# A norm tail shared by two engines, reordered loads and value parts, and a pause ahead of scatter and gather DMAs

## The reference

```
xn = layernorm(x)
s  = (sigmoid(LN(xn Wq + bq) LN(xn Wk + bk)^T / 16 - log 2048) (xn Wv + bv)) Wo + bo, times layerscale
f  = routed(xn) + shared(xn)      # 16 experts, top 4 of them per row after a choice of 2 groups of 4; shared: 2 x 128 wide
x  = x + s * silu(f)
xn = layernorm(x)
s  = gelu(sqrt(2048) * (xn K^T) / norm(xn K^T)) V           # bank of 2048 keys and values
f  = gelu(xn ternary(W1)^T + b1) ternary(W2)^T + b2
x  = x + s * silu(f)
```

## Time and profile before

| what | value |
|---|---|
| three runs | 1225.1, 1225.28, 1227.74 us; median 1225.28 |
| the profiled execution | 1224.77 us, span 1223.0 us |
| PE busy | 1193.8 us, 98% of the span |
| DVE, ACT, POOL busy | 69%, 45%, 35% |
| mean granted clock of TensorE | 0.995 |
| DMA | 169.14 MB, 138 GB/s |

### The profile page before, as it was taken

One profiled execution on the slowest core, in us unless ns is written; L12 is line 12 of the kernel. 1 busy time (PEld: TensorE's weight loads), 2 busy tenths in 40 slices (PEclk: granted clock), 3 DMA queues, 4 the chain that ended last, 5 costly groups with the idle time before them and its releaser, 6 DMA issues.

```text
span 1223.0 us, 26541 instructions
## 1 busy us (share of the span) xinstructions
PE 1193.8 (98%) x8888; PEld 853.5 (70%) x8889; DVE 845.1 (69%) x1821; ACT 555.4 (45%) x1054; POOL 426.4 (35%) x376
## 2 busy tenths in 40 slices
PE   5899999999999999999999999999999999999998
PEld 4566566676788888866666667777766666666665
DVE  8697966556556555578899899999765545554554
ACT  6545732333466666665333345677542222222221
POOL 3353777777027360055777752212000000000000
PEclk8999999999999999999999999999999999999999
DMA  9488355454297666522566647541111101101100
GB/s 297 169 340 326 114 163 178 159 188 132 78 286 241 199 194 193 171 83 74 150 212 199 183 151 234 171 139 53 53 52 53 34 19 53 52 8 43 52 18 18
DMA packets 137830, 169.14 MB, mean 138 GB/s; under 512 B 12899, under 2 KB 126710, under 8 KB 135446
## 3 DMA queue, kind: packets, MB, share of 16 engines
q1 hardware_dynamic: 114438, 125.49, 31.6%
q0 software_dynamic: 12368, 33.70, 8.7%
q10 hardware_dynamic: 10944, 8.92, 2.3%
HBM read 84.18 MB, written 83.89 MB: 137 GB/s over the span
## 4 chain that ended last, share of the span: by engine, by line
PE 81%; DVE 11%; issue 4%; ACT 2%; DVEq 1%; DMA 1%; SPq 0%; ACTq 0%
PE bank L1220 28%; PE sums L1276 17%; PE sums L1235 12%; PE bank L1139 8%; PE sums L1149 4%; PE bank L1081 3%; PE bank L1119 3%; DVE stat L1890 2%; PE sums L1091 1%; DVE reg_w L2169 1%; PE sums L1072 1%; PE bank L1184 1%; PE bank L1057 1%; DVE reg_e L2159 1%; DVEq L1893 1%
## 5 line engine op out<-in xcount | busy, mean ns | idle before, releaser
L2169 DVE TENSOR_SCALAR reg_w<-reg_w 128x512 f16<-128x512 f32 x320 | 147.2, 460 | 197.8 <-ACT reg_w L1664 196.9
L1845 DVE SCALAR_TENSOR_TENSOR reg_w<-reg_w 128x512 f16<-128x512 f32 x320 | 222.4, 695 | 11.0
L1276 PE MATMUL sums<-reg_v,reg_w 128*128 128x256 f16 x1536 | 188.3, 273 | 0.0
L1235 PE MATMUL sums<-reg_v,reg_w 128*128 128x256 f16 x1536 | 188.1, 273 | 0.1
L1220 PE MATMUL bank<-reg_qk 128*128 (+1 forms) x768 | 186.6, 379 | 0.0
L1220 PE MATMUL bank<-reg_qk,kbT 128*128 128x512 f16 (+1 forms) x768 | 186.6, 379 | 0.0
L1664 ACT ACTIVATE reg_w<-bank 128x512 f32<-128x512 f32 x128 | 76.4, 597 | 241.8 <-PE bank L1220 241.8
L1276 PEld LDWEIGHTS sums<-reg_v,reg_w 128*128 128x128 f16 x1536 | 150.3, 98 | 44.3
L1235 PEld LDWEIGHTS sums<-reg_v,reg_w 128*128 128x128 f16 x1536 | 150.1, 98 | 44.3 <-DVE reg_w L1845 1.1
L1664 ACT ACTIVATE reg_w<-bank,nlogs 128x512 f32<-128x512 f32 x128 | 87.9, 687 | 162.5 <-PE bank L1220 157.6
L864 POOL DMA_INDIRECT reg_e<-yg_d,slot_i x128 | 131.0, 1023 | 45.7 <-issue 34.7
(11 more groups left out here) (244 smaller groups left out, 1646.9 us busy)
## 6 DMA issues: line engine op xcount, KB each, us to landing
xg_d<-kbT SPq DMA_DIRECT2D x18, 1024.0 KB, 4.9
xin<-xg_d SPq DMA_DIRECT2D x72, 256.0 KB, 2.9
yg_d<-xr SPq DMA_DIRECT2D x72, 256.0 KB, 2.2
reg_qk<-in_L_attn_x_dram SPq DMA_DIRECT2D x8, 512.0 KB, 7.5
sh_d<-xin SPq DMA_DIRECT2D x16, 256.0 KB, 2.4
xr<-xn_d SPq DMA_DIRECT2D x32, 128.0 KB, 2.4
reg_e<-sh_d SPq DMA_DIRECT2D x32, 128.0 KB, 2.8
moe_d<-reg_e SPq DMA_DIRECT2D x32, 128.0 KB, 1.9
```

What stands on the lines that cost most here:

```text
L1235: mm = pe.matmul(sums[:, bass.ds((c & 1) * (2 * 512) + q * D, D)], (ah, al)[x][:, j % 4, q * P:(q + 1) * P], m.second(y, j), start=(j == 0 ...
L1276: mm = pe.matmul(a_bank[2 * i + q // 2][:, (q % 2) * D:(q % 2 + 1) * D], part[:, j % 4, q * P:(q + 1) * P], m.second(y, j), start=(j == 0 ...
L1845: ins = dve.scalar_tensor_tensor(out=out_ap, in0=in_ap, scalar=scale, in1=hi_ap, op0=ALU.mult, op1=ALU.subtract)
L2169: dve.tensor_scalar(ah[:, j % 4, :], att[:, j % 2, :], m.split, None, ALU.mult).then_inc(m.hi_done, 1)
```

## The change

Four edits:

1. Norm tail. Of chunk 7's four blocks ACT normalizes two, and DVE the other two (`last_norm`), between weight block 6 and chunk 6. The high and low parts of weight block 7 (wpT) come behind those of chunk 7, together with block 8 (`splits_of`). PE's `route(5)` comes behind the transposes of chunk 7, with `route(6)` and `route(7)`.
2. SP issues the load of chunk 3 ahead of Wo, Wv and bv.
3. In each batch's projection the low parts of v of tiles 14 and 15 come behind the loop.
4. POOL executes a semaphore increment (`tile_seen`, which nothing waits for) between a tile's wait and its four DMAs, in `scatter` and in `gather`.

```diff
+        splits_of = slots_of[:NCH - 2] + [[], [WP_SLOT, BIAS_SLOT]]
+        tile_seen = sem("tile_seen")
...
             load(st_wk, rows(a["L0_attn_Wk"]), "qk")
+            load_x_all(3)
             load(st_wo, rows(a["L0_attn_Wo"]), "o_v")
             load(st_wv, rows(a["L0_attn_Wv"]), "o_v")
             load(bvf[:, :], a["L0_attn_bv"].rearrange("(t p) -> p t", p=P), "vb", allow_slow_non_contiguous=True)
-            load_x_all(3)
...
             def scatter(c):
                 pool.wait_ge(xr_ld[c % 4], 16 * (c // 4) + 16)
+                pool.sem_inc(tile_seen, 1)
                 for k in range(TOPK):
                     scatter_row(c, k)
...
             def gather(c):
                 pool.wait_ge(cb_step, TOPK * (c - YR + 1) + CR)
+                pool.sem_inc(tile_seen, 1)
                 for k in range(TOPK):
                     gather_row(c, k)
...
-                if c:
+                if 0 < c < NCH - 2:
                     route(c - 1)
-            route(NCH - 1)
+            for c in range(NCH - 3, NCH):
+                route(c)
...
-                for m in range(G4):
+                for m in range(G4 if c < NCH - 1 else 2):
                     ins = act.activation(xn4[c % 4][:, m, :], x_all[:, c, m, :], ACT.Identity,
                                          bias=nmr[:, i, m:m + 1], scale=rstd[:, i, m:m + 1])
...
-                for s in slots_of[c]:
+                for s in splits_of[c]:
                     weights_hi(s)
...
+            def last_norm():
+                c = NCH - 1
+                i = c % 2
+                dve.wait_ge(ln["xn"], at(2 * c))
+                for m in (2, 3):
+                    ins = dve.tensor_scalar(xn4[c % 4][:, m, :], x_all[:, c, m, :], rstd[:, i, m:m + 1],
+                                            nmr[:, i, m:m + 1], ALU.mult, ALU.add)
+                ins.then_inc(ln["xn"], 1)
...
-                for s in slots_of[c]:
+                for s in splits_of[c]:
                     weights_lo(s)
+                if c == NCH - 3:
+                    last_norm()
...
-                def row_moments(t, i):
+                def row_moments(t, i, values=True):
                     dve.wait_ge(pj["mm"], at(first_t + t))
                     dve.wait_ge(pj["qkn"], at(first_t + t - 2))
                     moments(lambda m: s_bank[i % 4][:, m * D:(m + 1) * D], 2, i % 2, first_t + t, pj, EPS * QK_PS * QK_PS)
+                    if values:
+                        values_lo(t, i)
+
+                def values_lo(t, i):
                     dve.wait_ge(pj["vhi"], at(first_t + t))
...
                     if more or i < 2:
-                        row_moments(t + 2, i + 2)
+                        row_moments(t + 2, i + 2, more)
...
                 by(dve, S // P, 4, rows_lo)
+                for i in (2, 3):
+                    values_lo(S // P - 4 + i, i)
```

## The result

The change took 1223.79 us (median of 19 runs, 1223.12 to 1225.29), the kernel before 1225.28 (19 runs, 1224.82 to 1227.74): ratio 0.9982, 95% interval 0.9975 to 0.9989, faster by 1.3 to 3.1 us. The medians differ by 1.49 us and the two profiled executions by 1.30 (1224.77 to 1223.47). Forecast were 1.4 us and 1223.9. Ten of before's runs lie at 1224.8 to 1225.3 and nine at 1226.1 to 1227.7; of the change's, one lies above 1224.3. So the ratio, by which the gain is 2.2 us (0.0018 of 1226), says more than the medians.

A forecast was written before the change was run, and what follows sets the result against it. PE, busy for 98% of the span, was taken as the bound. Terms -1.4 + 0 + 0 + 0 from 1224.77 gave 1223.4 us profiled, 1223.9 as a median, with a range of 1222.0 to 1226.8.

The forecast's parts named there:

- Part 1: Norm tail: DVE's idle time filled and wpT's low part moved behind chunk 7's, forecast -1.4 us, bounds 0.6 to 1.6.
- the cut of 0.1 for a late PE: Norm tail: 0.1 us taken off the 1.49 us gain because chunk 7's high parts had only 0.1 to spare.
- Part 2: Opening loads: chunk 3 comes sooner, but DVE then waits for chunk 4; forecast 0, bounds -0.67 and 0.
- Part 3: Projection's end: moving the last two value tiles' low parts leaves holes on DVE; forecast 0, -0.84 to +0.1 per batch.
- Part 4: POOL's semaphore pause ahead of each tile's four scatter or gather DMAs: forecast 0, between -0.28 and +0.30 us each.
- the 0.30 that I had as the upper bound: POOL's scatters and gathers: most one pause was taken to cost, in us, if it pays a second DMA gap.
- the room that I had counted: Gathers: 3.4 us before DVE's use of rstd plus 3.4 in POOL's waits, less 0.84, to absorb pause lag.
- my formula: Gathers: pause lag added over 28 tiles, free up to (3.4 + 3.4 - 0.84) / 28 = 0.21 us each.
- The sign I named for a wrong forecast: POOL's gap at a tile's first DMA exceeding 0.5 us, one of three listed signs.
- gathers falling behind: Rival at DVE's shift: pauses of 0.30 us outrun the room by 2.4, time 1226.3 us; chance 9%.
- "lost gain" rival: A low-clock stretch falls on the shared expert's first matmuls, costing up to 1.7 us, time 1225.6; chance 14%.
- value and load rivals: Projection waits shrink, 1222.2 us, chance 12%; the earlier load of chunk 3 pays too, 1223.2 us, chance 8%.

The follow-up runs named there:

- e1: The norm tail edit alone on the kernel before: ratio 0.9994 (0.9973 to 1.0015).
- e7: The whole change run again, at a time when PE was held back: ratio 0.9912 to the kernel before (0.9878 to 0.9946).
- e9: The whole change with the semaphore instruction behind each gather tile's first DMA instead of ahead of it: ratio 0.9985 to the kernel before.
- e2: The kernel before with only chunk 3's load moved ahead of Wo, Wv and bv: ratio 1.0004 (0.9979 to 1.0030).
- e3: The kernel before with only the low parts of the last two value tiles moved behind the projection loop: ratio 0.9997 (0.9973 to 1.0020).
- e11: The whole change plus scatters waiting for the tile before last, gathers waiting for the tile before, and chunk 4 loaded behind chunk 3: 1297.82 us, ratio 1.0585.
- e6: The kernel before with only chunk 3's load moved ahead of Wo, Wv and bv, sent a second time: ratio 1.0013 (0.9996 to 1.0031).
- e12: The whole change plus each tile's scatter waiting until those of the tile before last have landed: 1224.13 us, ratio 0.9978 to the kernel before.
- e10: The whole change plus each tile's scatter waiting until those of the tile before have landed: 1316.07 us, ratio 0.9216 to the kernel before.
- e4: The kernel before with only the semaphore instruction added ahead of each tile's scatters and gathers: ratio 0.9934 (0.9906 to 0.9961).
- e8: The whole change without the semaphore instruction: ratio 1.0009 to the kernel before (0.9982 to 1.0036).

## Why the prediction was right

**Part 1, -1.4 us: right, in place and size.** The chain is 1.23 us shorter at 41.46 and again at 58.17; with chunk 4's statistics 0.19 us later in this one execution, the tail itself gave 1.42. One term was mis-sized: DVE's two norm operations took 0.72 us on the chain (0.74 busy) and not 0.56; the 128x255 operations of the earlier trace rows were too cheap a neighbour. The four low parts took 2.40 there instead of 2.50. Together that is 3.12 for 3.06, so the working without the cut of 0.1 for a late PE would have given 1.43. The cut was not needed in this execution, and too small in e1, e7 and e9: that 1.4 and 1.42 agree so closely is partly luck.

**Part 2, 0: right**, for the reason given: chunk 4's landing sets DVE's next step (17.45 before, about 17.65 after). e2 shows it alone.

**Part 3, 0: right**, the hole doesn't close, since DVE waits for ACT's high part (e3).

**Part 4, 0: right in the sum, wrong in its working.** I priced an instruction between two DMAs and found what I took: the gap stays 0.30, also at the first DMA of 26 of the 28 gather tiles. I missed that the tile's wait moves from the DMA to that instruction. At a blocked tile this costs 0.53 us of restart and 0.4 of slower DMAs, above the 0.30 that I had as the upper bound. It didn't matter because only the first tile was blocked, and the room that I had counted took the lag up: the waits for DVE at the later tiles fell from 5.5 us to 2.2, and the last gather's rstd began at 721.72, 0.62 sooner than before where all else was 1.3 sooner, with DVE's use 2.7 us behind its end instead of 3.4. So about 0.7 us of lag was left of the first tile's, inside the room, and none was added per tile as my formula had it. The sign I named for a wrong forecast, a gap above 0.5, did occur, in the restart of the blocked tile, without a cost to the end. That the pause gains 10 us while PE is held back was nowhere in the prediction.

**The rivals.** That gathers falling behind reach the end is right as a mechanism, and e11 shows the price to within 0.4 us at DVE's shift; the pause is far from it. The low clock of the "lost gain" rival exists, with 1.68 us where the rival had 1.7, but it fell on the other side. In the nine profiles with the tail none had it at the shared matmuls (in three it took 0.45 a little earlier); in the five without the tail one had (e6). It could be what sets before's nine runs at 1226.1 to 1227.7 apart, but one in five is no proof, and a larger share of before's runs lies up there: nine of 19, and with e11 and e12 eight of 9 and ten of 13. A late load of chunk 4 (e3: 1.6 us) and the step at 130 us (0.5 to 0.7, in e1 and e10 over 4) move runs as far. The value and load rivals fell.

**The number.** The prediction's 1.4 is what one traced execution of each kernel shows, 1.30. The runs say 2.2 (1.3 to 3.1) and, with e12, 2.5. The part above 1.3, some 0.9 us, is in no term of the sum and in no trace; the forecast median came out to 0.1 us because it started from 1225.28, which is the top of before's lower group. What share the low clock, the late load and the step have in it stays open, since only one execution of each kernel was traced.

## What to carry to other kernels

Work moved into another engine's idle time pays where the chain says so, and in full only if the engine behind it (here PE with its transposes) keeps pace: at the lower clock a third of the gain was lost. Ask of a wait which instruction it stands on, not only how many instructions there are: an instruction put behind a wait takes the wait over. Before adding a cost up over all steps, ask at which of them it is paid: here one restart was paid, and the waits of later steps took it up, while a wait for each step's landing was paid 28 times and came out at the end (e11). And when runs differ by more than the effect sought, trace more than one execution of each kernel.

## What the runs showed of the hardware

- DVE's norm, a TENSOR_SCALAR of 128x256 with two scalars per row, took 0.37 us (two in 0.74); the 128x255 ones of the earlier trace rows took 0.28.
- A semaphore instruction ahead of an indirect DMA is free while nothing blocks (0.30 both ways); after a block the DMA starts 0.81 us behind its releaser instead of 0.27 (27 tiles of e4 and e7 against 28 of e8 and e9).
- The Trainium skill, page Perfetto Trace Analysis, section DMA Instruction — SWDGE (GPSIMD), has the sequencer ready for the next instruction once it has pushed such a DMA into the wait queue. The trace agrees: in the change the second tile's semaphore instruction ran at 574.2, while the first tile's third gather ran (573.32 to 574.45) and ahead of its fourth (574.76), and the gap of 0.30 stayed.
- In nine of the kernels (e1 to e9) PE got one matmul through in 2.8 us (median from 165 to 295 us) while indirect scatters ran one behind the other at a pitch of 1.27, in e3 for instance:

```profile
205.44 0.37 PE L1235 MATMUL sums<-reg_v,reg_w 128*128 128x256 f16 x1 [2.43 <-issue]
205.84 0.96 POOL L847 DMA_INDIRECT xg_d<-xr,slot_i  x1 [0.30 <-issue]
207.10 0.96 POOL L847 DMA_INDIRECT xg_d<-xr,slot_i  x1 [0.30 <-issue]
208.24 0.37 PE L1235 MATMUL sums<-reg_v,reg_w 128*128 128x256 f16 x1 [2.43 <-issue]
```

  Letting one tile's four land before the next freed PE in that stretch (e10: busy for 148.00 of 148 us). What brings this on is open; the same chip had the kernel before at 1426.45 us with e7 to e10 and at 1226.63 with e12.
